# Two spilled pairs convolved again in the last pass of a residual block, and four pairs finished on VectorE

## The reference

```python
out = conv3x3(g, quantize_weight(w1, 8), b1)
out = relu(batchnorm(out, gamma1, beta1))      # mean and variance over all images
out = conv3x3(out, quantize_weight(w2, 8), b2)
out = batchnorm(out, gamma2, beta2)
result = x + relu(out + g)
```

## Time and profile before

| | |
|---|---|
| median of three runs | 535.89 us |
| the profiled execution | 533.88 us |
| its span, first to last instruction | 532.1 us |
| mean granted TensorE clock | 0.971 |
| PE busy | 481.6 us (91%) |
| VectorE (DVE) busy | 416.1 us (78%) |
| ScalarE (ACT) busy | 344.0 us (65%) |
| moved by DMA | 99.27 MB |

### The profile page before, as it was taken

One profiled execution on the slowest core, in us unless ns is written; L12 is line 12 of the kernel. 1 busy time (PEld: TensorE's weight loads), 2 busy tenths in 40 slices (PEclk: granted clock), 3 DMA queues, 4 the chain that ended last, 5 costly groups with the idle time before them and its releaser, 6 DMA issues.

```text
span 532.1 us, 21191 instructions
## 1 busy us (share of the span) xinstructions
PE 481.6 (91%) x9781; PEld 402.4 (76%) x9781; DVE 416.1 (78%) x613; ACT 344.0 (65%) x390; POOL 94.9 (18%) x153
## 2 busy tenths in 40 slices
PE   3999999999999999999999999999996855988780
PEld 1899999999999787899888989888884432544340
DVE  7999989999999757988988887788877851765550
ACT  3898899998999955765555556665514724764450
POOL 2027366666551500040000000000000000000000
PEclk9999999999999999999999999999998995998996
DMA  8834775433333000044333300000065999999998
GB/s 291 338 129 130 261 263 190 169 127 133 128 136 130 8 7 7 32 171 168 128 129 129 124 4 4 2 4 4 2 245 180 366 407 432 424 427 430 430 428 343
DMA packets 22529, 99.27 MB, mean 187 GB/s; under 512 B 6568, under 2 KB 9000, under 8 KB 17320
## 3 DMA queue, kind: packets, MB, share of 16 engines
q1 hardware_dynamic: 20816, 81.55, 40.4%
q10 hardware_dynamic: 1624, 16.36, 7.3%
HBM read 61.48 MB, written 35.50 MB: 182 GB/s over the span
## 4 chain that ended last, share of the span: by engine, by line
PE 75%; DMA 16%; DVE 4%; ACT 2%; issue 1%; SPq 0%; DVEq 0%
PE conv_ps L1051 71%; DMA split<-in_x_dram 6%; DMA slots<-in_x_dram 5%; DMA xa<-in_x_dram 4%; PE conv_ps L1140 3%; ACT conv_ps L636 1%; DMA out_dram<-split 1%; DVE slots L998 1%; DVE split L1006 1%; DVE slots L1001 1%; PE conv_ps L1014 1%; ACT split L475 0%; DVE gn_tup L727 0%; DVE slots L1006 0%; PE conv_ps L1049 0%
## 5 line engine op out<-in xcount | busy, mean ns | idle before, releaser
L1051 PE MATMUL conv_ps<-split,wmat 64*64 64x385 f16 (+3 forms) x9216 | 380.4, 324 | 1.2 <-ACT split L475 1.2
L1051 PEld LDWEIGHTS conv_ps<-split,wmat 64*64 64x64 bf16 x9216 | 342.8, 107 | 35.2 <-DVE wmat L710 1.4
L509 ACT ACTIVATE slots<-conv_ps,par,evac_scale 128x784 f32<-128x784 f32 x124 | 123.8, 999 | 94.1 <-PE conv_ps L1051 92.3
L1140 PE MATMUL conv_ps<-slots,wmat 128*128 128x392 f32 x224 | 79.7, 515 | 23.4 <-ACT conv_ps L636 23.4
L828 DVE BATCH_NORM_STATS2 bn_tup<-slots 128x6 f32<-128x392 f32 x166 | 81.9, 555 | 15.6 <-ACT slots L509 15.6
L1140 PEld LDWEIGHTS conv_ps<-slots,wmat 128*128 128x128 f32 x224 | 43.7, 198 | 59.5 <-issue 32.3
L727 DVE BATCH_NORM_STATS2 gn_tup<-slots 128x6 f32<-128x448 f32 x112 | 61.8, 612 | 0.9 <-DMA slots<-in_x_dram 0.9
L795 DVE TENSOR_TENSOR split<-slots,split 128x3136 f16<-128x3136 f32 (+4 forms) x36 | 57.2, 1608 | 3.5 <-ACT slots L489 0.9
L797 DVE SCALAR_TENSOR_TENSOR split<-slots,split 128x3248 f16<-128x3248 f32 (+3 forms) x18 | 53.6, 2978 | 2.3
L1006 DVE SCALAR_TENSOR_TENSOR slots<-conv_ps,split 128x784 f32<-128x784 f32 x28 | 27.3, 975 | 30.2 <-PE conv_ps L1140 30.2
L636 ACT ACTIVATE conv_ps<-split,skip_b,skip_s 128x784 f32<-128x784 f32 x28 | 26.9, 996 | 31.7 <-DMA split<-in_x_dram 25.6
(11 more groups left out here) (120 smaller groups left out, 256.8 us busy)
## 6 DMA issues: line engine op xcount, KB each, us to landing
slots<-in_x_dram SPq DMA_DIRECT2D x51, 392.0 KB, 5.4
out_dram<-slots SPq DMA_DIRECT2D x10, 1568.0 KB, 24.6
split<-in_x_dram ACTq DMA_DIRECT2D x5, 1568.0 KB, 15.4
slots<-in_x_dram SPq DMA_DIRECT2D x4, 1568.0 KB, 7.4
y_spill<-slots SPq DMA_DIRECT2D x3, 1624.0 KB, 7.1
slots<-y_spill SPq DMA_DIRECT2D x3, 1624.0 KB, 7.4
y_spill<-slots SPq DMA_DIRECT2D x3, 1568.0 KB, 5.8
split<-in_x_dram SPq DMA_DIRECT2D x3, 1568.0 KB, 8.8
```

Of the source, the lines that this page charges most:

```text
L509: nc.scalar.activation(dst, src, ACT.Identity, bias=bias, scale=scale, accum_out=total).then_inc(evacuated[ph], 1)
L1051: return nc.tensor.matmul(bank[:, r0:r1, w0:w1], lhs, rows[:, top + r0:top + r1, w0 + kx - 1:w1 + kx - 1], start=n == 0 and part is hi_all ...
L1140: mm = nc.tensor.matmul(sums_in(k)[:, h], diag, addend[:, h], start=False, stop=True, skip_group_check=True)
```

## The change

The names are those of the code after.

- `y2_spill` keeps one pair instead of three. The second sums of the other two (passes `AGAIN` = 7 and 10) are overwritten, and in the last pass they are computed again from `x`, which is loaded there anyway: both affines and both convolutions, with `hi` and `lo` parts as before (`make_act1`, `make_hi1`, `again_low1`, `again_round1`, `make_act2`, `again_low2`, `again_round2`). The first repeated convolution also computes one more row for each half, so that no copy between the halves is needed. The sums stay in PSUM; ScalarE scales them (`seed_again`) and TensorE adds the skip input from the 16-bit parts (`add_parts`, four 16-bit matmuls a quarter).
- Passes 5, 6, 8, 9 (`TWO_PASS`) leave the ring. Each is done in two halves: ScalarE `two_affine`, VectorE `sum_and_add` and `relu_and_add`.
- The order of the passes, their slots and their input buffers are new (`ORDER3`, `SLOT3`, `x3`). The one remaining reload is used in pass 15 and goes into the slot of pass 5.
- All loads, stores and the reload of the last pass are issued on SP; none on ScalarE's queue.
- The two diagonals move out of the first weight matrix, which is still needed; they and a third one are made by GpSimd. Small tiles share one tile, and some coefficients are added.

```diff
-    RELOAD_INTO = (0, 2, 3)
+    AGAIN = (7, 10)
+    RELOADED = NP - 1
+    ORDER3 = (SPILL, NP - 1, *range(SPILL + 1, SPILL + 6), 0, SPILL + 6, SPILL + 7, 1, *range(SPILL + 8, NP - 1), 2)
+    TWO_PASS = (0, 5, 6, 8, 9)
+    STORES = [PARTS0, 2, 2, 2, 1, 2, 2, 2, 2, 2, 2, 1, 1, 1, 2, 4]
...
+        x3 = [ap[:, 0:PIX] for ap in (
+            slots[:, FREE], halves[0], halves[1], xa, slots[:, FREE], xa, slot3(2), slot3(0), xa, slot3(2), slots[:, FREE],
+            halves[0], halves[1], xa, slot3(2), slot3(0))]
+        again1 = [ap.bitcast(F16)[:, 0:2 * PIX].rearrange("p (h m) -> p h m", h=2) for ap in (halves[0], slot3(3))]
...
# SP, the last pass
+            store_first()
+            store_ring(1)
+            wait_stored(0)
+            load(7)
+            store_ring(2)
+            store_ring(3)
+            wait_out(3)
+            load(5)
+            wait_stored(2)
+            load(6)
+            store_ring(4)
+            wait_out(4)
+            load(10)
+            store_two_pass(5)
+            wait_out(5)
+            load(8)
+            store_two_pass(6)
+            wait_out(6)
+            load(9)
+            wait_stored(5)
+            sp.wait_ge(y2_spilled, 16)
+            sp.dma_start(slot3(RELOADED)[:, 0:PIX], y2_spill).then_inc(y2_loaded, 16)
+            store_ring(7)
+            wait_out(7)
+            load(11)
+            load(12)
+            store_two_pass(8)
+            wait_out(8)
+            load(13)
+            store_two_pass(9)
+            wait_out(9)
+            load(14)
+            wait_stored(7)
+            load(15)
+            for u in range(10, NP):
+                store_ring(u)
...
# ScalarE
+            def make_act1(r):
+                sc.wait_ge(x3_loaded[AGAIN[r]], 16)
...
+            for u in (2, 3):
                 for k in range(NQ):
+                    seed(u, k)
+            make_act1(0)
+            seed(4, 0)
+            seed(4, 1)
+            make_hi1(0)
+            seed(4, 2)
+            seed(4, 3)
+            two_affine(5, 0)
+            two_affine(5, 1)
+            make_act2(0, 0)
+            two_affine(6, 0)
+            make_act2(0, 1)
+            two_affine(6, 1)
+            make_act2(0, 2)
+            make_act2(0, 3)
+            seed_again(0, 0)
+            make_act1(1)
+            seed_again(0, 1)
+            make_hi1(1)
...
# VectorE
+            finish(4, 0)
+            finish(4, 1)
+            again_low1(0)
+            finish(4, 2)
+            finish(4, 3)
+            for r in range(2):
+                u = (5, 8)[r]
+                for q in range(NQ):
+                    two_pass(u, q)
+                    again_low2(r, q)
+                for q in range(NQ):
+                    two_pass(u + 1, q)
+                    finish(AGAIN[r], q)
+                    if (r, q) == (0, 1):
+                        again_low1(1)
+            for u in range(11, NP):
+                dve.wait_ge(x3_loaded[u], 16)
+                for k in range(NQ):
+                    finish(u, k)
...
# TensorE
+            add_skip(IN_PSUM)
+            for u in (2, 3, 4):
+                add_sums(u)
+            for q in range(NQ):
+                again_round1(0, q)
+            again_round2(0, 0)
+            for q in range(1, NQ):
+                again_round2(0, q)
+                add_parts(0, q - 1)
+            again_round1(1, 0)
+            add_parts(0, 3)
+            for q in range(1, NQ):
+                again_round1(1, q)
+            again_round2(1, 0)
+            for q in range(1, NQ):
+                again_round2(1, q)
+                add_parts(1, q - 1)
+            add_parts(1, 3)
+            for u in range(11, NP):
+                add_sums(u)
```

More of the change, by code:

```diff
@@ L1142, in _, with add_sums @@
                     mm.then_inc(skip_added, 1)
+            def add_sums(u):
+                pe.wait_ge(scale_diag_ready, 2)
+                if u == RELOADED:
+                    pe.wait_ge(y2_loaded, 16)
+                for k in range(NQ):
+                    pe.wait_ge(seeded, nth(u, k))
+                    ys = banked(out_of(u), u, k)
+                    for h in range(2):
+                        mm = nc.tensor.matmul(sums_in(k)[:, h], scale_diag, ys[:, h], start=False, stop=True, skip_group_check=True)
+                    mm.then_inc(skip_added, 1)
@@ new lines, in again_round1 @@
+            def again_round1(r, q):
+                pe.wait_ge(again_hi1, r + 1)
+                pe.wait_ge(ring_out, nth((4, AGAIN[0])[r], q))
+                for part in range(2):
+                    if part == 1:
+                        pe.wait_ge(again_lo1, r + 1)
+                    for n in range(9):
+                        for a in range(2):
+                            for b in range(2):
+                                mm = again_tile1(r, q, part, n, a, b, n == 8 and part == 1)
+                mm.then_inc(again_conv1, 1)
@@ new lines, in again_round2 @@
+            def again_round2(r, q):
+                pe.wait_ge(again_lo2, NQ * r + q + 1)
+                for part in range(2):
+                    pe.wait_ge((again_hi2, again_lo2)[part], NQ * r + min(q + 2, NQ))
+                    for n in range(9):
+                        for a in range(2):
+                            for b in range(2):
+                                mm = again_tile2(r, q, part, n, a, b, n == 8 and part == 1)
+                mm.then_inc(again_conv2, 1)
+            add_skip(IN_PSUM)
```

407 lines of the change are left out of this document (283 added, 124 removed).

## The result

The changed kernel takes 549.08 us, median of 4 runs (548.32 to 549.53), against 536.08 us of the kernel before beside it: a ratio of 1.0239, 95% interval 1.0221 to 1.0256. It is slower, as forecast, but by 13 us and not by 4, and above the range. A second set of runs of the same kernel gave 549.86 us. The profiled execution took 549.53 us, with a span of 547.7 us; the forecast for that span was 536.4 us. So 11.3 us are to be found.

What follows compares the result with a forecast made beforehand. The DMA engines were taken to bound the last pass. 7.5 us saved, 12.8 us of empty queue and 1.0 us back gave 4.3 us more: span 536.4 us, 540.2 us against the median; 8-in-10 range 534.8 to 547 us.

Steps and rivals of the forecast that it cites:

- the range: Time against the median: 534.8 to 547 us, 8 in 10; the forecast proper, 537 to 544 us, had chance 0.66.
- the step that decides: Last pass: SP issues all transfers in order and waits for pass 6, leaving 12.8 us of empty queue.
- The bytes from 408 us on: Last pass: 46.6 MB moved from 408 us on, against 49.83 MB in the kernel before.
- The dip of the DMA share near 443 us: Last pass: a sign, DMA share under 1 around 443 and 454 us as the queue runs short.
- 471.6: Last pass: when VectorE finishes pass 6, so that SP can store its second half and issue further transfers.
- the slack: Slow stretch of 424 to 434 us: its 1.0 us was to fall into the queue's empty time.
- First repeated matmul: Last pass: PE starts the first repeated convolution at 440.0 us, after the adds of pass 4.
- rival (b): Repeated rounds: clock stays at 1.2 GHz, +5 to +12 us, 546 to 552 us; chance 0.16 shared with the slower-queue rival.
- the duration of a round from 387 to 399 us: Repeated convolutions: 11.87 us on PE per convolution of one pair, four of them 47.5 us.
- 64.8 us: After pass 6: 16.5 transfers of 1.606 MB still to move, 61.9 us at 428 GB/s, to a 536.4 us span.
- Rival (c): Rest of last pass: one queue moves only 381 GB/s, 548 us; chance 0.16 shared with the slow-clock rival.

Runs made afterwards that it cites:

- e3: Changed kernel with ScalarE's first two seeds of pass 4 moved ahead of make_act1(0): 546.99 us, ratio 1.0200.
- e5: Changed kernel with only taps 0 and 8 of nine run in the repeated convolutions: 544.17 us, ratio 1.0140.
- e7: Changed kernel with the stores of passes 3 to 6 writing only 64 columns of each piece: 542.72 us, one run.
- e1: Changed kernel with VectorE doing all four steps of passes 6 and 9 before the repeated pass's second finish: 543.19 us, ratio 1.0136.
- e6: Kernel before, with loads of passes 6 and later issued from SP instead of ScalarE: 536.39 us, ratio 1.0012.
- e14: Kernel before, with 48 extra stores of 392 KB beside the second convolution pass, four in flight: 535.50 us, ratio 0.9991.
- e8: Kernel before, with the stores of passes 4 to 13 split in two halves each: 536.22 us, ratio 1.0006.
- e16: Changed kernel with loads of passes 5, 6 and 8 to 13, the reload and store 4 in quarters by columns: 547.45 us, ratio 1.0215.
- after_again: The changed kernel itself, unedited, measured again: 549.86 us, ratio 1.0253.
- e9: Changed kernel with the outputs of passes 7 to 10 stored whole instead of in halves: 547.69 us, ratio 1.0225.
- e2: Changed kernel with SP issuing the reload and first half of store 7 ahead of the second half of store 6: 549.23 us, ratio 1.0258.
- e4: Changed kernel with VectorE ending pass 6 early, SP's reload and half store moved ahead, and ScalarE's seeds first: 541.05 us, ratio 1.0078.
- e15: Kernel before, with 48 extra stores of 392 KB beside the second convolution pass, all issued at once: 535.71 us, ratio 0.9998.

## Why the prediction was right in kind and wrong in size

**Right: the step that decides.** The forecast rested on SP, which issues nothing until pass 6 is done, on an empty queue before it, a full one after it, and VectorE done some 13 us before the end. All of it is there: a share of 0.07 at 474 to 480 us, a burst of issues from 479.26 us, VectorE's last operation at 533.5 us, 14 us before the end. The bytes from 408 us on are 46.96 MB (46.6 forecast). In `e3`, `e5` and `e7` the end moves with the issue of load 9 (rest 68.2, 68.7 and 67.6 us); in `e1`, where stops follow, only in part (72.1 us). The dip of the DMA share near 443 us is there (0.54); that of 454 us hardly (0.97).

**Wrong: its time, 478.85 instead of 471.6 us.** The 7.25 us, in order:
- The last pass starts 1.74 us later: the first affine at 408.02 us instead of 406.28. I had taken nothing for it. It is no cost of the change. It is there already in the second pass, at the operation of VectorE that the earlier trace rows has at 190.77 us: 192.51 us in the changed kernel, but 190.65 us in `e7`, and in profiles of the kernel before, which is unchanged up to there, 190.38 us (`e6`), 191.93 us (`e14`) and 192.75 us (`e8`, whose first affine is at 408.25 us). So profiles differ by that much with no edit before this point, and the one on which the forecast rests was an early one: its 533.88 us lie 2.0 us below the median, and all runs of the kernel before lie between 533.43 and 538.66 us. The forecast put these 2.0 us into the median, where they belong, and not into the span. Why executions differ stays open.
- Load 7 lands about 1.0 us later still: ScalarE starts `make_act1(0)` at 431.27 us, not 428.5. The queue moved 350 GB/s from 424 to 431.3 us, where I took 428 (the earlier trace rows had 381 to 387 GB/s; I put it into the slack).
- The adds of pass 4 ran at 1.2 GHz: the granted clock from 434 to 440 us is 0.50, behind a pause of 3.56 us, so their 16 matmuls take 8.21 us. From the end of ScalarE's last seed (440.85 us) to the first repeated matmul it is 2.6 us instead of 1.5, so 1.1 us of this lie on the path. I had kept it for the range. First repeated matmul at 443.5 us instead of 440.0, which contains the three terms (ScalarE's own instructions took 0.4 us less than forecast). From 444 to 504 us the clock is 1.00: rival (b), slow convolutions, is out.
- The first repeated convolution took 13.3 us instead of 12.3 (0.6 us is a stop), and from there to `finish(7, 1)` it was 13.5 us instead of 10.3 (1.9 us is a stop, and a round beside the full queue takes up to 3.56 us and not 2.97). Together 26.75 us instead of 22.6: 4.1 us, the largest term, and one that no step of the prediction had. This is the step that failed: I took the duration of a round from 387 to 399 us of the kernel before, where the DMA engines were not idle but no stop fell (a share of 0.71, 273 GB/s), for a stretch with large transfers in a full queue. `e7` gives the split: the same work takes 23.70 us when the queue is mostly free. So 3.05 us of the term are the queue's, 2.5 us of them in the two stops in which PE waits for instructions, and 1.1 us are not: there two rounds together take 6.30 us even in `e7` and `e16`, and the adds of `add_parts` 0.84 us instead of 0.7. `e16` gets back 2.6 of the 3.05 us by smaller transfers. (Against the 26.19 us of `after_again` the two figures are 2.5 and 2.1 us.)
- VectorE's last part took 8.65 us instead of 9.0.

**Wrong: what follows it, 68.8 instead of 64.8 us.** The bytes were right, the rate was not: 371 and 357 GB/s from 480 to 492 us, 421 GB/s later, where I took 428. By these rates 1.8 us are lost from 480 to 492 us and 0.8 us from there to 540 us; the other 1.4 us are at the two ends, above all in the last 7.7 us, which run at a share of 0.61 and 241 GB/s. Rival (c) named a slower single queue; `e6` rules that cause out (1.0012), and `e8` half stores beside the ring. `e9`, with whole stores, has 352 GB/s in the same 12 us. Why these run so slowly beside a full PE stays open. So this term was mis-sized by 4.0 us and its cause is not known.

**The sum.** 7.25 + 4.0 = 11.3 us, the whole distance between the spans of 536.4 and 547.7 us; the medians (540.2 and 549.08) are 2.4 us less apart, because I had added 2.0 us from the profiled run to the median, and now the median lies 0.45 us below the profiled run. The late start of 1.74 us is most of what these 2.0 us stood for, so against the medians 8.9 us are left, and the full queue beside PE is the largest known part. The time fell where rivals (b) and (c) had put it, 546 to 552 and 548 us, but neither cause was at work: that is coincidence.

**A rival not seen.** I asked whether the empty stretch could be avoided, and took an order of instructions as given. `e1` shows 6 us in the order of VectorE alone: the halves of pass 6 were done on time but for `again_low1` and two `finish` in front of them. Every such gain was in part given back, as stops (6.1 us in `e1`, 3.04 us at once in `e2`) or as a new empty stretch (506 us in `e2`, 454 us in `e4`).

## What to carry to other kernels

If one sequencer issues all transfers in order, find the instruction that it waits for last and sum the chain up to it; units saved behind it count for less than the time the queue stands empty before it. Durations of a dense matmul stream do not hold beside a full queue of large transfers if they were taken without one: take them from a stretch with the same DMA load, or add the stops. Look for "issue" among TensorE's waits; where it shows beside a full queue, and 128 matmuls with their weight loads lie between two such stops, PE waits for its instructions. Transfers of a quarter of the size took the stops away in `e15` and nearly all in `e16`; they cost rate, and in the changed kernel no gain in time was clear. And a profile is one execution: compare its span with the median before a span is forecast from it.

## What the runs showed of the hardware

- Twelve stores of 1.61 MB (rows of 12.5 KB) beside a convolution on PE, wanted by nobody, cost 12.5 us: 9.9 us in six stops, 7.0 to 7.6 us apart, and the rest in slower rounds, some 1.3 us of it at 1.2 GHz behind a stop of 2.24 us. The same bytes as 48 stores of 392 KB cost nothing, at 385 instead of 418 GB/s.
- Instructions come in packets of 16.4 KB, one in 5 us beside a convolution; beside the large stores one in 7.3 us. Between two of these stops lie 256 of PE's instructions, and each stop ends 1.4 to 1.5 us after a packet's end.
- One issuing queue does as well as two here (1.0012 [0.9997, 1.0028]).
- 3.56 us of pause before fp32 matmuls were followed by 1.2 GHz from 434 to 440 us, and the dense stream behind ran at 2.4 GHz.
